# A graph network's first dense layers in three node blocks of 418 columns in place of four of 314

## The chip, the core and the metric

The kernel runs on one core of a Trainium2 chip. The time is the device time of one execution in microseconds (us). Engines are named as the profile names them: PE is TensorE, PEld its weight loads, DVE VectorE, ACT ScalarE, POOL GpSimd, SP SyncE. Each engine runs its own list of instructions in order, and engines wait for each other by counters (semaphores).

## The reference

Two graph layers follow each other on 1250 nodes of 512 values and 20000 edges. The first is the one that the change touches:

```python
h = jnp.maximum(_layernorm(x, axis=-1), 0.0)
agg = jax.ops.segment_sum(h[src], dst, num_segments=N)
z = (1.0 + eps) * h + agg
z = jax.nn.relu(batch_norm(z @ W1 + b1, g1, be1))      # 512 -> 1024
z = jax.nn.relu(batch_norm(z @ W2 + b2, g2, be2))      # 1024 -> 512
x = x + (h + z)
```

`batch_norm` takes mean and variance of a feature over all nodes. The second layer normalises `x` again, forms for every edge a two-layer product of both end nodes and the edge's 64 attributes with `mish` behind each, sums the messages by target node, and ends in an update network over the nodes:

```python
h = mish(concatenate([h[src], h[dst], edge_attr]) @ W1 + b1)
agg = jax.ops.segment_sum(mish(h @ W2 + b2), dst, num_segments=N)
out = mish(concatenate([h, agg]) @ W3 + b3) @ W4 + b4
```

## The kernel before, in words

The program is written by hand, one list of instructions for each engine. Its stages in order of time: counts of the edges between each pair of nodes (to about 103 us of the span), the first layer's sum as a product with that count matrix (line 870, to 153.7), the first network's two products (line 952, 155 to 270), a short stretch to turn the result back to rows and normalise it, the products P and Q of the second layer (line 995, 280 to 338), the edge loop (to about 1050), and the update network.

In the first network features lie on partitions and nodes along the row, 1250 nodes padded to `NW` columns, cut in `BLOCKS` blocks of `BW` columns, each with a bank of PSUM of its own. Every factor is held as a high and a low part, so one product is three matmuls (high by low, low by high, high by high). `product_t` issues them. For the first output group of 128 features (o = 0) it goes by the inner dimension k, and for each k over all blocks, since its inputs are made one k after the other. For the others it takes one block after another, with all k in it, in two hardware loops. In the second product (4 outputs, 8 inner steps) `between` is called behind the first of the two loops: `transpose_back(o - 1)` turns the output before back to rows by ten transposes on PE (line 925), into banks 0 to 3.

ACT moves each finished block out of PSUM with its bias (`move_product`, L1190), takes the square root of a variance (L1180), and applies scale, shift and ReLU to a whole output (L1184). DVE takes the batch statistics of each moved block (`batch_norm`, L1539), sums them up (L1544), works out scale and shift in four small steps (L1549 to L1552), and behind the second block adds the transposed output before to `x` (`residual_early`, L1927). At the last output this call does more: ten statistics over the first 384 values of every row tile of `x` (L1936). Only then come the remaining blocks' statistics.

Hand-over from the first to the second product: the ReLU outputs are split by ACT (L1280, high) and DVE (L1909, low), and PE takes inner step k when the low part of k is there. Hand-over from the second product to rows: with no further output to hide it, the last output's move, statistics, scale, shift and ReLU (L1310, by blocks), its transposes (in groups of 2, 4 and 4 row tiles, `FILLS`), residual, row statistics (L1953, L1957) and normalisation (L1321) follow one another. PE runs 13 products whose result nobody reads before the first of these transposes, and 2, 4 and 7 further on (`idle_products`, L812).

The lines that set the order around the change:

```python
for o in range(1, on):
    for first, end in ((0, BLOCKS // 2), (BLOCKS // 2, BLOCKS)):
        with pe.Fori(first, end) as b:
            ...
        if between and first == 0:
            between(o - 1)
```

Of the kernel before, what the change touches and what calls it, by code (L numbers as in the profile page):

```python
# [17 lines left out]
ALU = mybir.AluOpType  # L18
# [8 lines left out]
P = 128  # L27
# [59 lines left out]
FINAL = EDGE_PAIRS - 1  # L87
assert EDGE_TILES == 2 * FINAL + 1 and FINAL % 2 == 0
SLOTS = 4
BLOCKS = 4  # L90

BW = -(-NODES // (2 * BLOCKS)) * 2
NW = BLOCKS * BW
assert NODES <= NW <= NP
LN_EPS = BN_EPS = 1e-5


# [17 lines left out]
def gnn_kernel(nc, x, src_cols, dst_cols, dst_rows, edge_attr_t, eps, cols, rows, w01, w02,  # L115
               w1, w2, w3, w4, out):
    ctx = ExitStack()
    with ctx:
# [59 lines left out]

        iota_at = place[0]
        IOTA, _ = sb("iota", [P, NP])  # L180
        XWORK_0, _ = sb("mish3_work_0", [P, 2, BW], at=iota_at)
        XWORK_1, _ = sb("mish3_work_1", [P, 2, BW], at=b2_at)
        XWORK = (XWORK_0[:, :, :], XWORK_1[:, :, :])
        assert place[0] <= nc.sbuf_usable_end

# [144 lines left out]
        UP_0, _ = sb("u_part_0", [P, 6, BW], at=wa_at + 4 * KD * DIM)  # L330
        UP_1, _ = sb("u_part_1", [P, 6, BW], at=wb_at + 4 * KD * DIM)
        UP_2, _ = sb("u_part_2", [P, 4, BW], at=rows_at)
        assert 4 * 6 * BW <= 4 * KD * DIM and 4 * 4 * BW <= 4 * 3 * DIM
# [122 lines left out]
        Z0_READY = (7, 7, 10, 12)  # L456
        SPREAD_ROWS = [(a, min(a + 512, NP)) for a in range(0, NP, 512)]
        MM_1 = 0
        FREE = 4
        MM_2 = BLOCKS * KH  # L460
        MM_PQ = MM_2 + BLOCKS * KD
        MM_UP = MM_PQ + 2 * NT
        MM_U = MM_UP + BLOCKS * KD
        TABLE_STORED = 16 * NT

        OUT_LAST = NT - 2
# [74 lines left out]
        def _(pool):  # L541
# [207 lines left out]
            def u_high(n):  # L749

                b, q = n // UPAIRS, n % UPAIRS
                at = (slice(2 * q, 2 * q + 2), slice(b * BW, (b + 1) * BW))
# [8 lines left out]


            pool.wait_ge(tr_done, TR_AG + NT)
            for n in range(UPAIRS * BLOCKS):
                u_high(n)
            for nt in range(OUT_LAST):
                finish(nt)
# [2 lines left out]
        def _(pe):  # L770
# [174 lines left out]
            def product_t(base, weights, acts, kn, on, ready, count, between=None):  # L945


                def terms(k, o, b):
                    bank = Z2[:, bass.ds(b, 1), 0:BW].rearrange("p o n -> p (o n)")
                    nodes = bass.ds(b * BW, BW)  # L950
                    for n, (w, a) in enumerate(((0, 1), (1, 0), (0, 0))):
                        mm = pe.matmul(bank, weights[w][:, k, o * P:(o + 1) * P], acts[a](k)[:, nodes],  # L952
                                       start=(k == 0 and n == 0), stop=(k == kn - 1 and n == 2), skip_group_check=True)
                    return mm

                for k in range(kn):
# [53 lines left out]
                pq(1, nt, q_moved, 0)  # L1010
            def u_terms(bank, high_w, low_w, high, low, o, b):

                nodes = slice(b * BW, (b + 1) * BW)
# [24 lines left out]
            def z2(s, j, k):  # L1038

                at, e = Z2[:, 2 * j + k, :], slice(k * P, (k + 1) * P)  # L1040
                if k == 0:
                    if after(s, 2):
                        pe.wait_ge(msg_full, s - 1)
                    else:
                        pe.wait_ge(up_moved, BLOCKS * KD)
# [51 lines left out]

            pe.wait_ge(w3a_lo, KD)
            pe.wait_ge(mm_moved, FREE + MM_PQ + NT)
            for b in range(BLOCKS):  # L1100
                for o in range(KD):
                    n = KD * b + o
                    if n == 2:
                        pe.wait_ge(q_moved, NT)
                    if n >= 4:
                        pe.wait_ge(up_moved, n - 3)
                    u_terms(Z2[:, n % 4, 0:BW], W3A_HI, W3A_LO, HT_HI, HT_LO, o, b)
# [17 lines left out]
            def y_product(nt):  # L1125

                if nt >= 4:
                    pe.wait_ge(y_moved, nt - 3)
                nodes = slice(nt * P, min((nt + 1) * P, NW))
                last_block = (nodes.stop - 1) // BW  # L1130
                for k in range(KD):
                    if k % 2 == 0:
                        pe.wait_ge(u_lo, UPAIRS * last_block + k // 2 + 1)
                    for n, (u, w) in enumerate(((U_LO, W4_HI), (U_HI, W4_LO), (U_HI, W4_HI))):
                        mm = pe.matmul(BANKS[0:nodes.stop - nodes.start, nt % 4, :], u[:, k, nodes], w[:, k, :],  # L1135
                                       start=(k == 0 and n == 0), stop=(k == KD - 1 and n == 2))
                mm.then_inc(y_done, 1)

            def u_product(b, q):


                pe.wait_ge(ag_lo, -(-(b + 1) * BW // P))
                if b > 0:
                    pe.wait_ge(u_bias, UPAIRS * (b - 1) + q + 1)
                for o in (2 * q, 2 * q + 1):
                    u_terms(Z2[:, o, 0:BW], W3B_HI, W3B_LO, AG_HI, AG_LO, o, b)

            def ag_t(nt):
                transpose_node(AGG, nt, ag_lo)
# [7 lines left out]
            u_product(0, 1)  # L1157
            ag_t(8)
            ag_t(9)
            for b in range(1, BLOCKS):  # L1160
                for q in range(UPAIRS):
                    u_product(b, q)
            pe.wait_ge(w4_lo, KD)
# [4 lines left out]
        def _(act):  # L1168
# [247 lines left out]
            for b in range(BLOCKS):  # L1416
                for o in range(KD):
                    n = KD * b + o
                    act.wait_ge(mm_done, MM_UP + n + 1)
                    if n == 12:  # L1420
                        act.wait_ge(rows_used, 2 * NT)
                    nc.scalar.activation(u_part(b, o)[:, 0, :], Z2[:, n % 4, 0:BW], ACT.Identity, bias=COLS[:, CB3 + o:CB3 + o + 1]).then_inc(up_moved, 1)
# [69 lines left out]
            u_log(0)  # L1492
            ag_high(9)
            u_inverse(0)
            for n in range(1, UPAIRS * BLOCKS):
                u_mish(n)
            for nt in range(NT):
                y_scale(nt)
# [2 lines left out]
        def _(dve):  # L1501
# [619 lines left out]
            dve.wait_ge(agg_done, SUMS1 + EDGE_GROUPS)  # L2121
            def u_at(n):
                b, q = n // UPAIRS, n % UPAIRS
                return slice(2 * q, 2 * q + 2), slice(b * BW, (b + 1) * BW)

            def u_start(n):

                b, q = n // UPAIRS, n % UPAIRS
                o, nodes = u_at(n)
                dve.wait_ge(mm_done, MM_U + KD * b + 2 * q + 2)  # L2130
                nc.vector.tensor_tensor(UT[:, o, nodes], Z2[:, o, 0:BW], u_part(b, 2 * q, 2), ALU.add).then_inc(u_bias, 1)

            def u_bound(n):

# [48 lines left out]
            u_bound(1)  # L2183
            ag_low(8)
            ag_low(9)
            for n in range(2, UPAIRS * BLOCKS):
# [56 lines left out]
```

## Time and profile before

| | us |
|---|---|
| median of three runs | 1128.69 |
| lowest and highest | 1127.28, 1129.93 |
| the profiled execution | 1129.61 |
| its span in the trace | 1127.6 |
| PE busy in it | 1066.4 |
| DVE, ACT, POOL busy | 871.6, 896.2, 656.1 |

The span is the stretch that the trace covers. The profiled execution's own time is 2.0 us longer than its span. PE is busy in 95% of the span. Shares of busy time are no limit by themselves: two matmuls in the pipeline overlap in the trace, since each is drawn from its start to the arrival of its last result, so the pace of PE is read from the distance of starts, not from the length of one.

### The profile page before, as it was taken

The numbers are of one execution on the slowest core, as the hardware profiler recorded it, in microseconds if no ns is written. First come the engines' busy times: TensorE is split into PE (matmuls) and PEld (weight loads), VectorE is DVE, ScalarE is ACT, GpSimd is POOL, SyncE is SP. The second block draws the span as 40 slices with busy tenths as digits, with TensorE's granted clock in tenths as the row PEclk, the third lists the DMA queues.
The fourth block names the chain that finished last, engine by engine and source line by source line (L and its number), as shares of the span: only waits on it lengthen the run. The fifth ranks groups of instructions, "written<-read, shape, count | busy, mean of one in ns | idle before, by whom it ended". The sixth has DMA issues, their size and how long they took to land.

```text
span 1127.6 us, 18568 instructions
## 1 busy us (share of the span) xinstructions
PE 1066.4 (95%) x5764; PEld 902.2 (80%) x5765; DVE 871.6 (77%) x1529; ACT 896.2 (79%) x1134; POOL 656.1 (58%) x549
## 2 busy tenths in 40 slices
PE   3568999999999999999999999999999999999997
PEld 1125889998888888888888888888888888888795
DVE  7999535536426388888889998998888888888786
ACT  5995745624503799999999999999999999999584
POOL 6765323002155576776888888888876677660227
PEclk9779999999999999999999999999999999999999
DMA  3003920301265386666666666666666666661002
GB/s 103 8 1 103 160 75 1 122 1 47 75 224 112 87 189 144 145 131 138 129 141 139 131 133 145 131 139 133 140 137 133 136 141 133 137 129 39 1 1 92
DMA packets 61087, 121.41 MB, mean 108 GB/s; under 512 B 7851, under 2 KB 18348, under 8 KB 60918
## 3 DMA queue, kind: packets, MB, share of 16 engines
q0 software_dynamic: 38048, 87.58, 38.3%
q1 hardware_dynamic: 22998, 33.32, 8.9%
q8 instruction: 21, 0.34, 0.1%
q14 instruction: 20, 0.16, 0.0%
HBM read 107.82 MB, written 7.80 MB: 103 GB/s over the span
## 4 chain that ended last, share of the span: by engine, by line
PE 86%; DVE 9%; ACT 2%; issue 2%; DVEq 1%; POOL 0%; ACTq 0%; POOLq 0%
PE banks L1054 12%; PE banks L1049 12%; PE banks L1050 12%; PE banks L952 10%; PE banks L1034 7%; PE banks L1074 6%; PE banks L1028 6%; PE banks L995 5%; PE banks L1016 4%; PE banks L870 4%; DVE edge_counts L1713 4%; PE banks L1047 3%; PE banks L1135 2%; DVE key_onehot L1660 1%; PE banks L925 1%
## 5 line engine op out<-in xcount | busy, mean ns | idle before, releaser
L688 POOL DMA_INDIRECT gather_pq<-q_table,dst x157 | 295.4, 1882 | 56.8 <-issue 47.5
L680 POOL DMA_INDIRECT gather_pq<-p_table,src x157 | 173.3, 1104 | 138.6 <-PE banks L1034 85.4
L1049 PE MATMUL banks<-w_lo,h_hi 128*128 128x512 f32 x620 | 241.5, 390 | 0.0
L1050 PE MATMUL banks<-w_hi,h_hi 128*128 128x512 f32 x620 | 241.3, 389 | 0.0
L1054 PE MATMUL banks<-w_hi,h_lo 128*128 128x512 f32 x620 | 166.2, 390 | 0.0
L1050 PEld LDWEIGHTS banks<-w_hi,h_hi 128*128 128x128 f32 x620 | 116.4, 188 | 24.8
L1054 PEld LDWEIGHTS banks<-w_hi,h_lo 128*128 128x128 f32 x620 | 116.4, 188 | 24.2
L2009 DVE SCALAR_TENSOR_TENSOR h_full<-mish_work,banks 128x512 f32<-128x512 f32 (+1 forms) x154 | 98.4, 681 | 46.6 <-ACT mish_work L1362 43.4
L1049 PEld LDWEIGHTS banks<-w_lo,h_hi 128*128 128x128 f32 x620 | 116.5, 188 | 21.9
L2034 DVE SCALAR_TENSOR_TENSOR message<-mish_work,banks 128x1024 f32<-128x1024 f32 x78 | 95.3, 1221 | 8.7 <-ACT mish_work L1386 0.7
L1350 ACT ACTIVATE mish_work<-banks 128x1024 f32<-128x1024 f32 (+1 forms) x77 | 78.6, 1021 | 26.4 <-PE banks L1034 26.3
L1034 PE MATMUL banks<-edge_attr_parts,we_hi 128*128 128x256 f32 (+1 forms) x316 | 94.6, 321 | 2.4 <-DVE edge_attr_parts L2002 2.4
L2044 DVE TENSOR_TENSOR message_lo<-message,message_hi 128x1024 fp32r<-128x1024 f32 x78 | 96.0, 1231 | 0.1
L1028 PE MATMUL banks<-ident,gather_pq 128*128 128x128 f32 x628 | 94.4, 272 | 0.3 <-DVE h_full L2009 0.2
L2023 DVE TENSOR_TENSOR h_lo<-h_full,h_hi 128x1024 fp32r<-128x1024 f32 (+1 forms) x77 | 93.3, 1211 | 0.0
L1382 ACT ACTIVATE mish_work<-mish_work 128x1024 f32<-128x1024 f32 (+1 forms) x79 | 83.4, 1055 | 2.5
L1028 PEld LDWEIGHTS banks<-ident,gather_pq 128*128 128x128 f32 x628 | 74.8, 140 | 11.1 <-DVE h_full L2009 0.6
L1358 ACT ACTIVATE mish_work<-mish_work 128x1024 f32<-128x1024 f32 (+1 forms) x77 | 81.4, 1057 | 2.4
L1354 ACT ACTIVATE mish_work<-mish_work 128x1024 f32<-128x1024 f32 (+1 forms) x77 | 81.3, 1056 | 2.5
L1386 ACT ACTIVATE mish_work<-mish_work 128x1024 f32<-128x1024 f32 (+1 forms) x79 | 83.1, 1052 | 0.1
L1378 ACT ACTIVATE mish_work<-mish_work 128x1024 f32<-128x1024 f32 (+1 forms) x79 | 82.4, 1044 | 0.1
L1034 PE MATMUL banks<-edge_attr_parts,we_lo 128*128 128x256 f32 (+1 forms) x316 | 81.8, 281 | 0.0
(269 smaller groups left out, 2686.2 us busy)
## 6 DMA issues: line engine op xcount, KB each, us to landing
edge_attr<-in_edge_attr_t SPq DMA_DIRECT2D x79, 128.0 KB, 3.5
x_nodes<-h_hi POOLq DMA_DIRECT2D x10, 256.0 KB, 13.4
x_nodes<-h_lo POOLq DMA_DIRECT2D x10, 256.0 KB, 7.9
p_table<-p_stage SPq DMA_DIRECT2D x10, 256.0 KB, 2.0
q_table<-agg_nodes SPq DMA_DIRECT2D x10, 256.0 KB, 3.9
gather_pq<-p_table,src POOLq DMA_INDIRECT x157, 3.9
gather_pq<-q_table,dst POOLq DMA_INDIRECT x157, 4.9
x_nodes<-in_x SPq DMA_DIRECT2D x3, 768.0 KB, 6.3
```

The lines of the kernel that those rows point to most:

```text
L680: nc.gpsimd.indirect_dma_start(GP[:, 2 * j + k, :], None, p_tab[:, :], bass.IndirectOffsetOnAxis(ap=SRC[:, 2 * s + k:2 * s + k + 1], axis= ...
L688: nc.gpsimd.indirect_dma_start(GP[:, 2 * j + k, :], None, q_tab[:, :], bass.IndirectOffsetOnAxis(ap=DST[:, 2 * s + k:2 * s + k + 1], axis= ...
L952: mm = pe.matmul(bank, weights[w][:, k, o * P:(o + 1) * P], acts[a](k)[:, nodes], start=(k == 0 and n == 0), stop=(k == kn - 1 and n == 2) ...
L1028: pe.matmul(Z1v[:, c, k * P:(k + 1) * P], GP[:, 2 * slot + k, c * P:(c + 1) * P], IDENT[:, :], is_transpose=True, skip_group_check=True, s ...
L1034: mm = pe.matmul(Z1v[:, c, 0:P * tiles(s)], w[:, c * P:(c + 1) * P], AT_R[:, j, 0:P * tiles(s)], skip_group_check=True, start=False, stop= ...
L1049: pe.matmul(at, h_high(s, j)[:, c, e], W2_LO[:, c, :], start=False, stop=False)
L1050: pe.matmul(at, h_high(s, j)[:, c, e], W2_HI[:, c, :], start=False, stop=False)
L1054: mm = pe.matmul(at, h_low(s, j)[:, c, e], W2_HI[:, c, :], start=False, stop=(c == KD - 1))
L2009: nc.vector.scalar_tensor_tensor(h_full_of(s)[:, at[0], at[1]], z1_work(s)[:, at[0], at[1]], -0.5, Z1v[:, at[0], at[1]], ALU.add, ALU.mult ...
L2023: nc.vector.tensor_tensor(h_low(s, j)[:, :, 0:P * tiles(s)], h_full_of(s)[:, :, 0:P * tiles(s)], h_high(s, j)[:, :, 0:P * tiles(s)].bitcas ...
L2034: nc.vector.scalar_tensor_tensor(MSG[:, :, :], EB[:, :, :], -0.5, z2_out(s, j), ALU.add, ALU.mult).then_inc(msg_full, 1)
L2044: nc.vector.tensor_tensor(MSG_LO[:, :, :], MSG[:, :, :], MSG_HI[:, :, :].bitcast(F32), ALU.subtract).then_inc(msg_lo, 1)
```

## The change

`BLOCKS` is now 3, `BW` 418 and `NW` 1254 for the first network and its input. The update network at the end keeps four blocks of 314 under new names, `UBLOCKS` and `UBW`. The two hardware loops of an output cover blocks 0 and 1, and block 2; the transposes stand between them. ACT's early split of a hidden output, which `BLOCKS // 2` places, now comes behind block 1.

```diff
-BLOCKS = 4
-
-BW = -(-NODES // (2 * BLOCKS)) * 2
+BLOCKS, UBLOCKS = 3, 4
+BW, UBW = (-(-NODES // (2 * n)) * 2 for n in (BLOCKS, UBLOCKS))
 NW = BLOCKS * BW
-assert NODES <= NW <= NP
+assert NODES <= NW <= UBLOCKS * UBW <= NP
...
-        FREE = 4
+        FREE = BLOCKS
...
-        MM_U = MM_UP + BLOCKS * KD
+        MM_U = MM_UP + UBLOCKS * KD
...
-                    for first, end in ((0, BLOCKS // 2), (BLOCKS // 2, BLOCKS)):
+                    for first, end in ((0, BLOCKS - 1), (BLOCKS - 1, BLOCKS)):
                         with pe.Fori(first, end) as b:
```

The remaining lines of the diff put `UBW` and `UBLOCKS` where the update network used `BW` and `BLOCKS`. Lines of the changed kernel stand one further down.

On DVE, at the last output of the second product, behind the scale and shift of the output before. `act_t` is the second product's result, `x_nodes` the rows. Before:

```order
L1539 BN_STATS bn_stats<-act_t 128x6 x2
L1927 TENSOR_TENSOR x_nodes<-x_nodes,banks 128x2x128
L1927 TENSOR_TENSOR x_nodes<-x_nodes,banks 128x4x128 x2
L1936 BN_STATS stats<-x_nodes 128x6 x10
L1539 BN_STATS bn_stats<-act_t 128x6 x2
L1544 BN_AGGR bn_mean_var<-bn_stats 128x2
L1549 RECIPROCAL tmp<-tmp 128x1
```

In the changed kernel:

```order
L1540 BN_STATS bn_stats<-act_t 128x6 x2
L1928 TENSOR_TENSOR x_nodes<-x_nodes,banks 128x2x128
L1928 TENSOR_TENSOR x_nodes<-x_nodes,banks 128x4x128 x2
L1937 BN_STATS stats<-x_nodes 128x6 x10
L1540 BN_STATS bn_stats<-act_t 128x6
L1545 BN_AGGR bn_mean_var<-bn_stats 128x2
L1550 RECIPROCAL tmp<-tmp 128x1
```

The order stays: residual and ten row statistics behind the second block's statistics. Behind them stand one block's statistics where there were two, so the run of thirteen instructions is now directly ahead of the last block.

On ACT, at the same place: the last moves, the splitting of the next layer's weights, the square root, and the ReLU by blocks. Before:

```order
L1190 ACTIVATE act_t<-banks,cols 128x314 x3
L1297 CAST w_hi<-weights_a 128x512 x2
L1180 ACTIVATE tmp<-bn_mean_var,consts 128x1
L1297 CAST w_hi<-weights_a 128x512 x2
L1310 ACTIVATE act_t<-act_t,bn_shift,bn_scale 128x314 x4
```

In the changed kernel:

```order
L1191 ACTIVATE act_t<-banks,cols 128x418 x2
L1298 CAST w_hi<-weights_a 128x512 x2
L1181 ACTIVATE tmp<-bn_mean_var,consts 128x1
L1298 CAST w_hi<-weights_a 128x512 x2
L1311 ACTIVATE act_t<-act_t,bn_shift,bn_scale 128x418 x3
```

One move and one ReLU piece fewer stand there, and each of the others is a third wider.

## Rows read from the trace of the kernel before

**Rows 1.** The page, part 1: busy time, share, instructions, by engine.

```profile
PE 1066.4 (95%) x5764; PEld 902.2 (80%) x5765; DVE 871.6 (77%) x1529; ACT 896.2 (79%) x1134; POOL 656.1 (58%) x549
```

**Rows 2.** Chain of waits by time, 150:345: start us, us, engine and line, count.

```profile
155.35 60.93 PE banks L952 x420
...
216.29 15.95 PE banks L952 x108
...
233.34 13.83 PE banks L952 x96
...
305.99 32.71 PE banks L995 x144
```

**Rows 3.** Timeline of PE, 152:155.5: start us, us, operation, shapes.

```profile
152.14 0.27 PE L870 MATMUL banks<-counts_hi,h_hi 128*128 128x232 f32 x1
...
152.58 0.40 PE L870 MATMUL banks<-counts_hi,h_hi 128*128 128x512 f32 x1
...
153.05 0.39 PE L870 MATMUL banks<-counts_hi,h_hi 128*128 128x512 f32 x1
...
155.35 0.38 PE L952 MATMUL banks<-z_t_lo,w_hi 128*128 128x314 f32 x1 [1.67 <-DVE z_t_lo L1869]
```

**Rows 4.** Groups by form, 155:273 and 155:275: count, busy us, mean ns, idle before.

```profile
L1539 DVE BATCH_NORM_STATS2 bn_stats<-hidden_t 128x6 f32<-128x314 f32 x24 | 11.2, 482 | 11.7 <-ACT hidden_t L1190 11.7
...
L1936 DVE BATCH_NORM_STATS2 stats<-x_nodes 128x6 f32<-128x384 f32 x10 | 4.7, 545 | 0.0
...
L1190 ACT ACTIVATE hidden_t<-banks,cols 128x314 f32<-128x314 f32 x32 | 16.2, 519 | 23.8 <-PE banks L952 23.8
L1184 ACT ACTIVATE hidden_t<-hidden_t,bn_shift,bn_scale 128x1256 f32<-128x1256 f32 x8 | 11.5, 1434 | 2.4 <-DVE bn_shift L1552 2.4
```

**Rows 5.** Timeline between the two products, 204:232, PE and DVE.

```profile
210.85 0.30 PE L952 MATMUL banks<-hidden_lo,w_hi 128*128 128x314 f32 x1
...
214.78 7.12 DVE L1909 TENSOR_TENSOR hidden_lo<-hidden_t,hidden_hi 128x1256 fp32r<-128x1256 f32 x5
```

**Rows 6.** Timeline, 262:264.8: the last output's transposes on PE.

```profile
261.92 1.25 PE L925 MATMUL banks<-ident,act_t 128*128 128x128 f32 x10
```

**Rows 7.** Timeline of DVE, 262:276.

```profile
262.67 0.49 DVE L1539 BATCH_NORM_STATS2 bn_stats<-act_t 128x6 f32<-128x314 f32 x1 [2.08 <-ACT act_t L1190]
...
264.71 4.70 DVE L1936 BATCH_NORM_STATS2 stats<-x_nodes 128x6 f32<-128x384 f32 x10
269.33 0.47 DVE L1539 BATCH_NORM_STATS2 bn_stats<-act_t 128x6 f32<-128x314 f32 x1
270.65 0.48 DVE L1539 BATCH_NORM_STATS2 bn_stats<-act_t 128x6 f32<-128x308 f32 x1 [0.85 <-ACT act_t L1190]
271.16 0.26 DVE L1544 BATCH_NORM_AGGREGATE bn_mean_var<-bn_stats 128x2 f32<-128x24 f32 x1
```

**Rows 8.** Timeline of ACT, 269:276.

```profile
270.09 0.52 ACT L1190 ACTIVATE act_t<-banks,cols 128x314 f32<-128x314 f32 x1 [2.92 <-PE banks L952]
...
271.54 0.29 ACT L1180 ACTIVATE tmp<-bn_mean_var,consts 128x1 f32<-128x1 f32 x1
...
272.77 2.27 ACT L1310 ACTIVATE act_t<-act_t,bn_shift,bn_scale 128x314 f32<-128x314 f32 x4
```

**Rows 9.** Timeline of PE, 269:281.

```profile
269.89 3.16 PE L812 MATMUL banks<-b_parts,ones 128*128 128x512 f32 x13
273.47 0.44 PE L925 MATMUL banks<-ident,act_t 128*128 128x128 f32 x2 [0.42 <-ACT act_t L1310]
```

**Rows 10.** Stretches of PE: length, busy (instructions), granted clock, DMA share, GB/s.

```profile
155.30:158.70 3.40, 3.35 (x23) 1.00 1.00 351
...
353.50:356.90 3.40, 3.40 (x16) 0.50 0.94 227
356.90:360.30 3.40, 3.40 (x25) 1.00 0.73 170
```

**Rows 11.** Timeline of PE, 349:357: the hole ahead of them.

```profile
352.10 0.39 PE L1034 MATMUL banks<-edge_attr_parts,we_hi 128*128 128x256 f32 x1 [2.44 <-DVE edge_attr_parts L2002]
```

More of the change, by code:

```diff
@@ L180, in gnn_kernel @@
         IOTA, _ = sb("iota", [P, NP])
-        XWORK_0, _ = sb("mish3_work_0", [P, 2, BW], at=iota_at)
-        XWORK_1, _ = sb("mish3_work_1", [P, 2, BW], at=b2_at)
+        XWORK_0, _ = sb("mish3_work_0", [P, 2, UBW], at=iota_at)
+        XWORK_1, _ = sb("mish3_work_1", [P, 2, UBW], at=b2_at)
         XWORK = (XWORK_0[:, :, :], XWORK_1[:, :, :])
@@ L329, in gnn_kernel @@
         W3B_HI, W3B_LO = W3_HI[:, 0, :, :], W3_LO[:, 0, :, :]
[L330 to L333, printed above, removed]
+        UP_0, _ = sb("u_part_0", [P, 6, UBW], at=wa_at + 4 * KD * DIM)
+        UP_1, _ = sb("u_part_1", [P, 6, UBW], at=wb_at + 4 * KD * DIM)
+        UP_2, _ = sb("u_part_2", [P, 4, UBW], at=rows_at)
+        assert 4 * 6 * UBW <= 4 * KD * DIM and 4 * 4 * UBW <= 4 * 3 * DIM
         UT, _ = sb("u_t", [P, KD, NP], at=t1_at)
@@ L751, in u_high @@
                 b, q = n // UPAIRS, n % UPAIRS
-                at = (slice(2 * q, 2 * q + 2), slice(b * BW, (b + 1) * BW))
+                at = (slice(2 * q, 2 * q + 2), slice(b * UBW, (b + 1) * UBW))
                 pool.wait_ge(u_ready, n + 1)
@@ L763, in _ @@
             pool.wait_ge(tr_done, TR_AG + NT)
-            for n in range(UPAIRS * BLOCKS):
+            for n in range(UPAIRS * UBLOCKS):
                 u_high(n)
@@ L1011, in u_terms @@
             def u_terms(bank, high_w, low_w, high, low, o, b):
-                nodes = slice(b * BW, (b + 1) * BW)
+                nodes = slice(b * UBW, (b + 1) * UBW)
                 for k in range(KD):
@@ L1044, in z2 @@
                     else:
-                        pe.wait_ge(up_moved, BLOCKS * KD)
+                        pe.wait_ge(up_moved, UBLOCKS * KD)
                     pe.wait_ge(h_hi, s + 1)
@@ L1099, in _ @@
             pe.wait_ge(mm_moved, FREE + MM_PQ + NT)
-            for b in range(BLOCKS):
+            for b in range(UBLOCKS):
                 for o in range(KD):
@@ L1106, in _ @@
                         pe.wait_ge(up_moved, n - 3)
-                    u_terms(Z2[:, n % 4, 0:BW], W3A_HI, W3A_LO, HT_HI, HT_LO, o, b)
+                    u_terms(Z2[:, n % 4, 0:UBW], W3A_HI, W3A_LO, HT_HI, HT_LO, o, b)
                     if n in Z1_BEHIND:
@@ L1128, in y_product @@
                     pe.wait_ge(y_moved, nt - 3)
-                nodes = slice(nt * P, min((nt + 1) * P, NW))
-                last_block = (nodes.stop - 1) // BW
+                nodes = slice(nt * P, min((nt + 1) * P, UBLOCKS * UBW))
+                last_block = (nodes.stop - 1) // UBW
                 for k in range(KD):
@@ L1139, in u_product @@
             def u_product(b, q):
-                pe.wait_ge(ag_lo, -(-(b + 1) * BW // P))
+                pe.wait_ge(ag_lo, -(-(b + 1) * UBW // P))
                 if b > 0:
@@ L1145, in u_product @@
                 for o in (2 * q, 2 * q + 1):
-                    u_terms(Z2[:, o, 0:BW], W3B_HI, W3B_LO, AG_HI, AG_LO, o, b)
+                    u_terms(Z2[:, o, 0:UBW], W3B_HI, W3B_LO, AG_HI, AG_LO, o, b)
             def ag_t(nt):
@@ L1159, in _ @@
             ag_t(9)
-            for b in range(1, BLOCKS):
+            for b in range(1, UBLOCKS):
                 for q in range(UPAIRS):
@@ L1415, in _ @@
             act.wait_ge(q_stored, TABLE_STORED)
-            for b in range(BLOCKS):
+            for b in range(UBLOCKS):
                 for o in range(KD):
@@ L1421, in _ @@
                         act.wait_ge(rows_used, 2 * NT)
-                    nc.scalar.activation(u_part(b, o)[:, 0, :], Z2[:, n % 4, 0:BW], ACT.Identity, bias=COLS[:, CB3 + o:CB3 + o + 1]).then_inc(up_moved, 1)
+                    nc.scalar.activation(u_part(b, o)[:, 0, :], Z2[:, n % 4, 0:UBW], ACT.Identity, bias=COLS[:, CB3 + o:CB3 + o + 1]).then_inc(up_moved, 1)
                     for s, first in enumerate(Z1_BEHIND):
@@ L1494, in _ @@
             u_inverse(0)
-            for n in range(1, UPAIRS * BLOCKS):
+            for n in range(1, UPAIRS * UBLOCKS):
                 u_mish(n)
@@ L2123, in u_at @@
                 b, q = n // UPAIRS, n % UPAIRS
-                return slice(2 * q, 2 * q + 2), slice(b * BW, (b + 1) * BW)
+                return slice(2 * q, 2 * q + 2), slice(b * UBW, (b + 1) * UBW)
             def u_start(n):
@@ L2130, in u_start @@
                 dve.wait_ge(mm_done, MM_U + KD * b + 2 * q + 2)
-                nc.vector.tensor_tensor(UT[:, o, nodes], Z2[:, o, 0:BW], u_part(b, 2 * q, 2), ALU.add).then_inc(u_bias, 1)
+                nc.vector.tensor_tensor(UT[:, o, nodes], Z2[:, o, 0:UBW], u_part(b, 2 * q, 2), ALU.add).then_inc(u_bias, 1)
             def u_bound(n):
@@ L2185, in _ @@
             ag_low(9)
-            for n in range(2, UPAIRS * BLOCKS):
+            for n in range(2, UPAIRS * UBLOCKS):
                 u_end(n - 2)
```

## The prediction

> **What bounds the kernel now.** I read the page first: PE is busy for 95% of the span [rows 1], so the question in each stage is only whether PE waits. Then the chain of waits over the changed stage, where the reader is to see that it runs through PE's line 952 almost without a break from 155.35 to about 270 [rows 2]. Inside the two products PE is the bound; DVE and ACT lie beside it. Three places are different: the start (PE waited 1.67 us for the last stage's result [rows 3]), the seam between the products, and the end, where nothing is left for PE and a chain of ACT and DVE steps decides. So the change is weighed as pace of the matmuls, plus what happens at the seam and at the end. Behind them P and Q follow with PE in the chain [rows 2], so a shift at the end is handed on whole.
>
> **The pace.** The columns stay: four blocks of 314 are 1256, three of 418 are 1254. The matmuls fall. First product: 8 outputs x 4 inner steps x 3 terms is 96 for each block, second: 4 x 8 x 3, again 96. So 192 groups of four matmuls become groups of three. One of 314 columns takes 13.83 / 96 = 144.1 ns from start to start, one of 512 takes 32.71 / 144 = 227.2 ns [rows 2]. At the granted full clock of 2.4 GHz the columns alone would be 130.8 and 213.3 ns; both sizes pay 13 to 14 ns beside them. No row has 418 columns. On the line between the two, 418 lies at 144.1 + 104 x (227.2 - 144.1) / 198 = 187.7 ns. A group is then 563.1 in place of 576.4 ns, 13.3 ns less, and 192 of them save **2.5 us**. The other end is line 870: 152.14 to 152.58 holds four of 232 columns, 110 ns each, 152.58 to 153.05 two of 512, 235 ns each [rows 3]. A straight line through these gives 193 ns at 418, a group of 579 ns, and the change would lose 0.5 us. I take the first, since lines 952 and 995 share the form (two parts by two parts, all in one bank for a whole run) while 870 goes from bank to bank. Range of the term: gain 2.7 (all of the fixed part plus two columns) to loss 0.5. Smaller: the input's last part is 230 wide, not 232, in 80 matmuls at (235 - 110) / 280 = 0.45 ns a column, 0.07 us gained. The hardware loops have one pass fewer for each output; the 96 matmuls of four passes ran at 144.1 ns, passes included, so I give that nothing.
>
> The Trainium skill, "TensorE: Matmul & The Clock Gate", section "Back-to-back issue gap", gives N / 2.4 GHz + 2.5 ns as the isolated distance when warm. By that the fixed part of a matmul would be a fifth of what these rows show, and 192 groups would save 192 x (2.5 + 0.8) ns, an estimate of 0.6 us, in place of 2.5. The trace differs with its 144.1 and 227.2 ns, and I go by the trace.
>
> **Banks.** Three banks serve where four did. The tightest use is at o = 1, where block 0 is wanted right behind o = 0. Its last matmul starts seven starts earlier, 1.3 us, its move starts 0.34 us behind that start (as 269.89 less 0.14 and 270.09 show [rows 8, 9]) and takes 0.62, so about 0.3 us are left. This cover is work of PE on the other two blocks; were it gone, it would cost up to 0.3 us twice. Elsewhere a bank has two blocks of at least 2.2 us as cover. Nothing for this. ACT's early split, about as long as the ReLU of 1434 ns [rows 4], follows this behind block 1 and delays the third move by about 1 us in two outputs, and that bank is not wanted for 4 us. Nothing either.
>
> **Wider pieces.** A move of 314 columns takes 519 ns, the ReLU over 1256 takes 1434 [rows 4], so 0.97 ns a column, and a piece of 418 takes 0.10 us more. Statistics: 482 ns at 314, 545 at 384 [rows 4], 0.90 ns a column, 0.09 to 0.10 us more at 418. While PE is the bound this is hidden. At seam and end it is not.
>
> **The seam.** PE starts the second product at 210.85 [rows 5] and reaches inner step 3 after 36 matmuls, at 216.04 by its pace. It really starts there at 216.29 [rows 2], because the fourth low part, the first of the five from 214.78 at 7.12 / 5 = 1.42 us each [rows 5], ends at 216.20. So PE lost 0.25 us. In the new kernel PE is there after 27 x 187.7 = 5.07 us, 0.12 earlier, and the low part comes 0.10 later, since the last move is longer and the split queues behind it on ACT. PE loses 0.47 in place of 0.25: **0.22 us lost**. The later low parts come each 1.42 us, PE wants one each 1.69, so they catch up.
>
> **The end.** This is where most is given back. Take as zero the start of the last output's transposes, 261.92 [rows 6]. DVE takes the second block's statistics at +0.75, then three residuals and from +2.79 to +7.49 the ten row statistics [rows 7]. The third block's statistics wait behind them until +7.41 and the fourth's start at +8.73, with DVE free [rows 7]: today the batch fits beneath two blocks of PE, 48 matmuls. In the new kernel it has to fit beneath one, 24 matmuls.
> New, from the same zero: PE takes 1.05 us for transposes (7.97 to the idle products [rows 9] less 48 x 0.1441) and 24 x 0.1877 = 4.51 for the last block, so it is done at +5.56 (call it E). The last move starts at E + 0.20 as today [rows 8, 9], and its statistics could start 0.56 + 0.10 later, at +6.42. DVE's batch starts 0.20 later than today (a wider move and wider statistics ahead) and frees DVE at +7.61. The last statistics wait **1.19 us**, in order on DVE. Behind them nothing is hidden. Today the square root starts 0.89 us after them [rows 7, 8]; the statistics are 0.10 longer, and some 0.07 falls away, since the root stands behind ACT's weight split and starts 0.12 after the sum's end at 271.42 [rows 7, 8], and that split will be long over. So the root starts at +8.53. The ReLU follows 1.23 us later [rows 8], and the transposes 0.70 after that [rows 8, 9], plus 0.10 for its wider first piece. Sum: transposes at +10.56, that is E + 5.00. Today they start at 273.47, 3.58 us after 269.89 [rows 9]. **1.42 us lost.** From there the path goes in order on DVE, with the same instructions. The second and third groups of transposes come earlier, as three pieces of ReLU are shorter than four, but DVE is not ready for them: no gain. POOL's weight split starts by the same signal, later by as much, and stays beneath the row statistics and the normalisation, which are later by as much too.
>
> **Sum.** -2.5 - 0.07 + 0.22 + 1.42 = -0.93 us. Made against the profiled execution's 1129.61 it gives 1128.68 (its span of 1127.6 would be 1126.7). That execution lies 0.9 us above the median of the three, 1128.69, and the same difference taken off the median gives **1127.8 us**. What can be told from no change by measuring this kernel is 0.2%, or 2.3 us, more than the sum.
>
> **Rivals.** *The gain comes whole* (chance 0.12). Were DVE's batch no obstacle, only the pace and the wider pieces would count, -2.5 - 0.07 + 0.22 + 0.25: 1126.6. For it speaks that PE's busy share is 95%; against it that DVE's list is in order and the batch stands ahead of the last block by the listing of both kernels.
> *The clock falls at the end* (0.18), the one that ends slower. PE's 13 idle products end 3.16 us after E today, and the hole behind them is 0.42 us [rows 9]. It would grow to 5.00 - 3.16 = 1.84 us. The trace has a hole of 1.67 us after which the clock stayed at 1.00 [rows 3, 10] and one of 2.44 us [rows 11] after which it was granted at 0.50, 1.2 GHz, for 3.4 us, in which PE started 16 matmuls where 25 followed in the next stretch [rows 10]. The new hole lies between. The work near it is partly idle products and transposes, but the seven idle products ahead of P are on the path. Price up to 1.7 us, half of 3.4: 1127.8 + 1.7 = 1129.5. It decides from a hole somewhere between 1.67 and 2.44 us on; against it speaks that 1.84 is nearer to the harmless one.
> *The pace is proportional to columns* (0.10). If what stands beside the columns grows with them (144.1 / 314 = 0.459 ns a column), a group saves 0.9 ns, or by line 870 loses 3, and seam and end still cost their 1.64: +1.4 to +2.1, 1130.1 to 1130.8. The small fixed part of the page named above would come out near it, at -0.6 - 0.07 + 1.64, or 1129.7.
> *The forecast* has 0.55. Left over, 0.05, is a stall that I do not see, in the banks first.
>
> **How the numbers follow.** The forecast's own range is 1127.0 to 1128.6. The range that is to hold 8 in 10 takes in the clock rival and most of the whole gain, and about 1 us for the runs' own scatter (1127.28 to 1129.93): 1126.0 to 1130.2. Faster by over 0.2% (below 1126.4) needs the whole gain and some luck: 0.13. Slower by over 0.2% (above 1130.9) needs pace and clock both wrong: 0.06. Within: 0.81.
>
> **What would show it.** In the changed profile: line 953 at 187 to 188 ns from start to start (192 would be the third rival); no wait of PE for ACT's move; the first wait for the low part at inner step 3 of about 0.5 us; ten statistics of x ending about 1.9 us after the last of line 953, the last block's statistics right behind them with no idle time before; PE idle for about 1.8 us ahead of the first transposes; the granted clock there at 1.00 (0.50 is the second rival). The prediction is wrong if DVE stands idle ahead of the last statistics, or if the end takes 3.8 us as today.

## The result and the profile after

The changed kernel takes 1131.95 us (median of 14 runs, 1129.99 to 1133.29) beside 1128.90 us for the kernel before (14 runs): ratio 1.0027, 95% interval 1.0019 to 1.0035. It is 3.05 us slower, by 0.27%, which lies above the predicted range of 1126.0 to 1130.2. The profiled execution took 1131.98 us, with a span of 1129.9.

The trace says where the time went. The table takes each stage from the start of its first matmul to the start of its last, or of the next stage's first.

| us | before | after | forecast | found |
|---|---|---|---|---|
| first layer's sum (L870) | 50.69 | 50.96 | -0.07 | +0.27 |
| first network (L952) | 114.40 | 113.80 | -2.28 | -0.60 |
| its end, to the first product P (L995) | 10.51 | 11.70 | +1.42 | +1.19 |
| products P and Q | 58.26 | 58.29 | 0 | +0.03 |
| edge loop (L1049), first to last | 673.86 | 675.96 | 0 | +2.10 |
| update network | 70.31 | 70.32 | 0 | +0.01 |

The rows add up to 3.00 us, beside 3.05 between the medians. Two stretches are left out, because they change from one profile to the next whatever the kernel. The counting stage ends, and the first layer's sum starts, at 102.59 us before and at 103.23 after, and between 101.3 and 103.4 in the profiles of all kernels below but e7, which adds work there. Between Q and the edge loop the profile of before has the clock at 0.50 for 3.4 us [rows 10], and that of after has not, which shortens this one profile by 1.37 us. Of the kernels below, e1, e2, e5, e6, e7, e10 and e11 have that fall, e3, e8, e9 and e12 do not.

**Two thirds of the loss lie where no line of code was changed**, in the edge loop.

The page says of PE what it said before [rows 1], and gives no hint of this:

```profile
PE 1066.8 (94%) x5572; PEld 894.8 (79%) x5573; DVE 871.1 (77%) x1517; ACT 894.1 (79%) x1121; POOL 657.6 (58%) x549
```

The chain of waits of the changed kernel, 150 to 345 us (start, length, engine and line, count), answers to [rows 2]:

```profile
156.25 55.33 PE banks L953 x288
...
212.12 1.25 ACT hidden_hi L1281
...
215.51 1.39 DVE hidden_lo L1910
216.95 18.04 PE banks L953 x93
...
236.08 13.77 PE banks L953 x72
...
250.94 13.79 PE banks L953 x72
...
307.48 32.74 PE banks L996 x144
```

The piece at 236.08 has the pace: 13.77 / 72 = 191.3 ns for 418 columns, where the sum had 187.7. In the middle the chain leaves PE, as forecast: the low part of inner step 3 is late. The waits of PE's weight loads between 205 and 235 us (total, times, longest), first of the kernel before, then of the changed one:

```profile
PEld banks L952 <- DVE hidden_lo L1909: 0.3, 1, 0.3
```

```profile
PEld banks L953 <- DVE hidden_lo L1910: 0.7, 2, 0.4
```

The end, on DVE and ACT of the changed kernel (timeline; idle time and its releaser in brackets), beside [rows 7, 8]:

```profile
265.39 0.60 DVE L1540 BATCH_NORM_STATS2 bn_stats<-act_t 128x6 f32<-128x418 f32 x1 [3.11 <-ACT act_t L1191]
...
267.54 4.70 DVE L1937 BATCH_NORM_STATS2 stats<-x_nodes 128x6 f32<-128x384 f32 x10
272.15 0.58 DVE L1540 BATCH_NORM_STATS2 bn_stats<-act_t 128x6 f32<-128x414 f32 x1
```

```profile
274.26 1.99 ACT L1311 ACTIVATE act_t<-act_t,bn_shift,bn_scale 128x418 f32<-128x418 f32 x3
```

The last block's statistics follow the ten row statistics with no idle time, although ACT had moved their block by 271.05. On PE (beside [rows 9]) and in the stretches with the granted clock (third number from the right; beside [rows 10]):

```profile
270.25 3.13 PE L813 MATMUL banks<-b_parts,ones 128*128 128x512 f32 x13
275.05 0.44 PE L926 MATMUL banks<-ident,act_t 128*128 128x128 f32 x2 [1.67 <-ACT act_t L1311]
```

```profile
272.50:275.05 2.55, 0.88 (x5) 1.00 1.01 386
275.05:278.50 3.45, 2.84 (x16) 1.00 0.21 48
```

PE was idle for 1.67 us ahead of the first transposes, and the granted clock stayed at 1.00, the level of 2.4 GHz. It stayed there too behind a longer hole, the one that answers to [rows 11], here with the stretch behind it:

```profile
353.63 0.39 PE L1035 MATMUL banks<-edge_attr_parts,we_hi 128*128 128x256 f32 x1 [2.59 <-DVE edge_attr_parts L2003]
```

```profile
353.90:357.30 3.40, 3.40 (x28) 1.00 1.00 195
```

A hole of 2.44 us was followed by 0.50 in the kernel before [rows 10, 11], and one of 2.59 us was not in the changed one. So the length of the hole does not decide by itself.

The edge loop. One of its lines, first and last start, of the kernel before and of the changed one:

```profile
L1049 PE MATMUL banks<-w_lo,h_hi x620: 387/389/398, 383.0 to 1049.2; 128*128 128x512 f32 x155
```

```profile
L1050 PE MATMUL banks<-w_lo,h_hi x620: 387/389/398, 383.2 to 1051.4; 128*128 128x512 f32 x155
```

666.2 us have become 668.2, and the single matmul is no longer than it was (387/389/398 ns, lowest, median, highest). What PE's weight loads wait for in 376:1049, before and after:

```profile
PEld banks L1028 <- DVE h_full L2009: 0.6, 1, 0.6
PEld banks L1028 <- issue: 0.5, 1, 0.5
```

```profile
PEld banks L1029 <- issue: 6.0, 20, 0.5
PEld banks L1029 <- DVE h_full L2010: 4.2, 18, 0.6
```

And DVE's sequencer, the register load in its loop (lowest, median, highest ns), before and after:

```profile
L1565 DVEq TENSOR_LOAD <-tile_range x39: 744/749/760, 388.5 to 1048.4; - x39
```

```profile
L1566 DVEq TENSOR_LOAD <-tile_range x38: 744/754/875, 388.6 to 1035.7; - x38
```

It hardly ever varied before; now it takes up to 875 ns. In 17 passes it stands at 799 to 875, the 3rd to the 9th and the 27th to the 36th, and PE has its 18 waits for DVE's `h_full`. Over the 35 passes from 409 to 1018 us the loads took 26.2 us before and 27.7 after, so they alone are 1.5 us longer. So DVE's sequencer is slower there, with the same instructions. The clock is no part of it: it was granted at 1.00 through the whole loop in both profiles.

### The profile page after: what moved, and what is told of

Same layout as the page of the kernel before. It is cut to its first block, busy times and chain, and to the rows that moved or that the text cites. A ratio compares the mean times of both kernels' runs of the same rounds, so it can differ in the third digit from the quotient of the medians.

```text
span 1129.9 us, 17891 instructions
## 1 busy us (share of the span) xinstructions
PE 1066.8 (94%) x5572; PEld 894.8 (79%) x5573; DVE 871.1 (77%) x1517; ACT 894.1 (79%) x1121; POOL 657.6 (58%) x549
## 4 chain that ended last, share of the span: by engine, by line
PE 85%; DVE 10%; ACT 2%; issue 2%; DVEq 1%; POOL 0%; ACTq 0%; POOLq 0%
PE banks L1050 12%; PE banks L1055 12%; PE banks L1051 12%; PE banks L953 9%; PE banks L1035 7%; PE banks L1075 6%; PE banks L1029 6%; PE banks L996 5%; PE banks L871 4%; PE banks L1017 4%; DVE edge_counts L1714 4%; PE banks L1048 3%; PE banks L1136 2%; DVE key_onehot L1661 1%; PE banks L926 1%
## 5 line engine op out<-in xcount | busy, mean ns | idle before, releaser
L681 POOL DMA_INDIRECT gather_pq<-p_table,src x157 | 176.7, 1125 | 137.0 <-PE banks L1035 83.8
L1351 ACT ACTIVATE mish_work<-banks 128x1024 f32<-128x1024 f32 (+1 forms) x77 | 78.6, 1021 | 28.4 <-PE banks L1035 28.4
L1029 PEld LDWEIGHTS banks<-ident,gather_pq 128*128 128x128 f32 x628 | 72.4, 140 | 15.2 <-issue 6.0
L1375 ACT ACTIVATE mish_work<-banks 128x1024 f32<-128x1024 f32 (+1 forms) x79 | 79.2, 1002 | 3.3 <-PE banks L1055 3.3
```

The lines of the kernel that those rows point to most:

```text
L681: nc.gpsimd.indirect_dma_start(GP[:, 2 * j + k, :], None, p_tab[:, :], bass.IndirectOffsetOnAxis(ap=SRC[:, 2 * s + k:2 * s + k + 1], axis= ...
L1029: pe.matmul(Z1v[:, c, k * P:(k + 1) * P], GP[:, 2 * slot + k, c * P:(c + 1) * P], IDENT[:, :], is_transpose=True, skip_group_check=True, s ...
```

## Experiments

Two things could make an untouched loop slower: where its data lie (the statistics buffer shrank from 24 to 18 numbers an output, and all buffers behind it moved), or where its instructions lie in an engine's list (ahead of the loop DVE has 12 instructions fewer, ACT 13, and PE, in the output groups that are written out one by one, 36 matmuls with their weight loads). Lengths of the stages in us, from the same starts as above; medians are of the runs, beside those of the kernel before on the same chip. e6, e7, e11 and e12 ran once, for their profile, so that their times are no basis for a ratio:

| | L870 | first network | end | edge loop | median (before) | ratio |
|---|---|---|---|---|---|---|
| before | 50.69 | 114.40 | 10.51 | 673.86 | 1128.90 | 1 |
| after | 50.96 | 113.80 | 11.70 | 675.96 | 1131.95 (1128.90) | 1.0027 |
| e1 | 50.69 | 114.38 | 10.52 | 673.90 | 1129.08 (1129.03) | 1.0002 |
| e2 | 50.96 | 113.77 | 11.71 | 675.81 | 1132.12 (1129.03) | 1.0035 |
| e3 | 50.95 | 113.78 | 10.67 | 676.11 | 1130.36 (1129.03) | 1.0014 |
| e5 | 50.95 | 114.18 | 11.68 | 673.84 | 1129.74 (1128.95) | 1.0006 |
| e6 | 50.96 | 113.77 | 11.69 | 675.85 | 1132.49, one run | |
| e7 | 50.96 | 114.02 | 11.70 | 676.03 | 1139.04, one run | |
| e8 | 50.98 | 113.77 | 10.66 | 673.84 | 1128.07 (1128.95) | 0.9992 |
| e9 | 50.72 | 113.12 | 11.73 | 676.12 | 1130.86 (1129.06) | 1.0015 |
| e10 | 50.73 | 112.35 | 10.66 | 673.76 | 1127.54 (1129.06) | 0.9986 |
| e11 | 50.69 | | | 676.85 | 1144.64, one run | |
| e12 | 50.68 | | | 673.79 | 1139.64, one run | |

**e1 and e2, the place of the buffers.** e1 is the kernel before, with the buffers where the change puts them:

```diff
-        BSTATS, _ = sb("bn_stats", [P, KH, 6 * BLOCKS])
+        place[0] += 4 * KH * 18
...
+        BSTATS, _ = sb("bn_stats", [P, KH, 6 * BLOCKS])
```

> The kernel before with four blocks of 314, but every buffer behind the batch statistics moved down by 192 bytes, to where the changed kernel has it (the statistics themselves stand at the end). The changed kernel's profile loses 2.1 us in the edge loop, whose code is the same. If the place of the buffers (the iota row, the small tables) does that, this kernel is 1.5 to 2.5 us slower than before and its edge loop (first product of line 1049's group to its last) takes about 676 us. If not, it is within 0.5 us of before and the loop takes about 674.

Measured: edge loop 673.90, ratio 1.0002 (0.9992 to 1.0013). e2 is the changed kernel with a statistics buffer as wide as before:

```diff
-        BSTATS, _ = sb("bn_stats", [P, KH, 6 * BLOCKS])
+        BSTATS_WIDE, _ = sb("bn_stats", [P, KH, 6 * UBLOCKS])
+        BSTATS = BSTATS_WIDE[:, :, 0:6 * BLOCKS]
```

> The changed kernel with a statistics buffer as wide as before, so that no later buffer moves. By the theory of the place it gains 2 us on the changed kernel and is about 1 us slower than before (ratio 1.001), loop 674 us. If the place is not the cause, it is like the changed kernel, 3 us slower than before (ratio 1.0027), loop 676 us.

Measured: 675.81, ratio 1.0035 (1.0024 to 1.0047). The place of the buffers is not the cause.

**e3, the end.** The changed kernel with seven of the ten row statistics ahead, and three where DVE waits for ACT anyway, behind the last scale and shift:

```diff
-                    for nt in range(NT):
...
+                    early_rows(0, ROWS_AHEAD)
...
+            early_rows(ROWS_AHEAD, NT)
```

> The changed kernel with seven of the ten row statistics ahead of the last block's statistics and three behind the last scale and shift. If these ten hold the last block back by 1.2 us, the time from the last of the second product's matmuls to the first of P falls from 11.7 us to 10.6, and the kernel is about 1.1 us faster than the changed one. If the end is longer for another reason (wider pieces, transposes), it falls by less than 0.4 us.

Measured: the end takes 10.67 for 11.70 us, the ratio is 1.0014 (1.0004 to 1.0024). DVE and PE of e3:

```profile
267.34 3.32 DVE L1934 BATCH_NORM_STATS2 stats<-x_nodes 128x6 f32<-128x384 f32 x7
270.89 0.59 DVE L1540 BATCH_NORM_STATS2 bn_stats<-act_t 128x6 f32<-128x414 f32 x1 [0.23 <-ACT act_t L1191]
...
272.85 1.47 DVE L1934 BATCH_NORM_STATS2 stats<-x_nodes 128x6 f32<-128x384 f32 x3
```

```profile
273.80 0.44 PE L926 MATMUL banks<-ident,act_t 128*128 128x128 f32 x2 [0.62 <-ACT act_t L1311]
```

Now DVE is free 0.23 us before the last block is moved, where in the changed kernel the block waited for DVE. The predicted mechanism is shown; the edge loop stays at 676.11, so the two are separate.

**e4, the pace by itself.** Only groups of matmuls of the form of L952 at sixteen widths and places, the rest of the computation left out.

> Leaves the whole computation out and runs only groups of matmuls (high and low part by rounded values) at sixteen widths and offsets, all else idle. The changed kernel's matmuls of 418 columns start 191.3 ns apart in the mean, not 187.7. If that is a matter of where rows begin or end in steps of 64 bytes (16 columns), 416 columns at multiples of 416 run at 186 to 187 ns and 418 at 191. If it is the neighbours (ACT and DVE at work), 418 runs at 187.7 here, as on the straight line. If every width that is no multiple of 128 or so has a rest of its own, 416 and 420 stand at 190 too, and 314 above its line.

Measured, mean ns from start to start, blocks side by side as in the kernel:

| columns | 256 | 314 | 320 | 384 | 416 | 418 | 420 | 424 | 448 | 480 |
|---|---|---|---|---|---|---|---|---|---|---|
| ns | 119.9 | 144.2 | 146.7 | 173.4 | 187.8 | 191.0 | 190.3 | 192.2 | 202.9 | 215.3 |
| less columns / 2.4 GHz | 13.2 | 13.4 | 13.3 | 13.4 | 14.4 | 16.8 | 15.3 | 15.5 | 16.2 | 15.3 |

With all blocks at offset 0, 418 takes 189.9 ns. The chain over the stretches of 416 and of 418 columns:

```profile
76.20 13.51 PE banks L175 x72
```

```profile
89.71 13.75 PE banks L175 x72
```

So the 191 ns of the network are the matmul's own, not the work of its neighbours, of which this kernel has none. The line from 314 to 512 columns (13 to 14 ns beside the columns at both ends) holds up to 384. Between 416 and 480 a matmul pays 1 to 3.5 ns more than that, and 418, of all widths tried, the most. These means mix paces: group by group (twelve matmuls into one bank) this one trace has 186.5 to 189.8 ns at 416 columns, where the line has 186.7, 189.5 to 192.5 at 418, and 186.7 to 191.9 at 420. So a difference of 1 ns between two widths says little; the 3.2 between 416 and 418 is clear. For 418 about 1 ns goes with the offset (189.9 with all blocks at 0) and the rest with the width; why is open.

**e5, e6, e7, the place in the list.** Small operations whose result nobody reads move the edge loop of one engine down its list: e5 twelve one-number copies on DVE ahead of the second `batch_norm` and e6 thirteen on ACT, which puts each loop back to where it stood; e7 98 matmuls of two columns on PE in the first stage, which need not be PE's old place.

```diff
+            for k in range(12):
+                nc.vector.tensor_copy(PAD[0:1, 16 + k:17 + k], CONST[0:1, 1:2])
```

> The changed kernel with twelve copies of one number on DVE ahead of the second product's statistics, where DVE is idle, so that DVE's edge loop stands at the same place of its instruction list as before (the change took twelve statistics out of the list). If the edge loop's extra 2.1 us comes from where DVE's loop stands in its instruction list, the loop takes 673.9 us again, DVE's register load of line 1565 takes 0.75 us throughout, and the kernel is 2 us faster than the changed one. If the cause is ACT's list or PE's, or the state in which the loop begins, the loop still takes about 676.

> The changed kernel with thirteen copies of one number on ACT ahead of the second product's moves, so that ACT's edge loop stands where it stood before in its list. Loop 673.9 us if ACT's place is the cause, about 676 if DVE's or PE's is.

> The changed kernel with 98 matmuls of two columns on PE in the counting stage, where PE is mostly idle, which brings PE's edge loop back to about the place in its list that it had before. Loop 673.9 us if PE's place is the cause, about 676 if not.

Measured: e5 673.84 us, e6 675.85, e7 676.03. With e5 the median falls to 1129.74, ratio 1.0006 (0.9997 to 1.0015). PE's waits in e5's loop and DVE's register load read like those of before:

```profile
PEld banks L1030 <- DVE h_full L2013: 0.6, 1, 0.6
PEld banks L1030 <- issue: 0.6, 2, 0.5
```

```profile
L1567 DVEq TENSOR_LOAD <-tile_range x38: 745/750/764, 390.1 to 1035.1; - x38
```

The cause is DVE's list: twelve instructions that do nothing useful take 2.1 us out of the loop, with PE's and ACT's lists left as in the changed kernel. e6 has the same extra buffer as e5 and stays slow, so it is not the buffer. (e7's total means nothing for this, since its own matmuls lengthen the first stage.)

**e11, e12, is it the place modulo 256?** The Trainium skill, "Runtime: NRT & Kernel Launch", section "Instruction fetch mechanics", says that an engine's instruction memory is refilled in blocks of 256 instructions and that a taken branch to a target outside the two blocks at hand has to fetch it. It also calls block crossings mostly hidden. If blocks of 256 are what counts, the kernel before must get slow with its loop 244 instructions further down (12 less than 256) and stay fast with 256.

```diff
+            for k in range(244):
+                nc.vector.tensor_copy(PAD[0:1, k:k + 1], CONST[0:1, 1:2])
```

> The kernel before with 244 one-number copies on VectorE ahead of the second normalization, which puts its edge loop 244 instructions further down in VectorE's list: a whole number of 256 further than in the changed kernel, where the loop took 676.0 us. Theory (the place modulo 256 instructions decides): the edge loop takes 675.5 to 676.1 us and the register load at its head 0.80 to 0.88 us in many steps. Rival (not the place, but that twelve statistics had gone or what they stood beside): 673.9 us and 0.75 us. Only the edge loop is read; the copies themselves lengthen the part ahead of it.

> The kernel before with 256 such copies at the same place, the control of the kernel with 244: the same load on VectorE ahead of the loop, but the loop stands at the same place modulo 256 instructions as in the kernel before. Theory: edge loop 673.8 to 674.0 us, register load 0.75 us. If the number of instructions ahead or any large shift slows the loop: about 676 us, as with 244.

Measured: e11 676.85 us, e12 673.79. PE's waits in e11, then in e12:

```profile
PEld banks L1029 <- issue: 6.5, 20, 0.5
PEld banks L1029 <- DVE h_full L2012: 4.7, 18, 0.6
```

```profile
PEld banks L1029 <- DVE h_full L2012: 0.6, 1, 0.6
PEld banks L1029 <- issue: 0.6, 2, 0.5
```

The register load, e11 and e12:

```profile
L1566 DVEq TENSOR_LOAD <-tile_range x38: 744/757/985, 400.5 to 1048.5; - x38
```

```profile
L1566 DVEq TENSOR_LOAD <-tile_range x38: 744/749/764, 398.5 to 1043.4; - x38
```

e11 has the changed kernel's waits, 20 and 18 of them, with four blocks of 314 columns, and its load is slow in the same passes. Twelve copies more, and they are gone. e11 came 0.75 us above its expected interval, and why is not known; the verdict does not hang on it. With e5 this settles that the place of DVE's loop in its list decides, and that the effect is back after 256 instructions; a period that divides 256 would fit these runs as well. What DVE's sequencer waits for is open. A fetch of instructions in every slow pass would fit the block length that the Trainium skill gives, but the records do not support it: the trace has the packets of two instruction queues (q8 and q14), and from 425 to 570 and from 820 to 1010 us of the changed kernel, where the slow passes are, there is none. From 376 to 1070 us both kernels have the same 11 of them. Whether these two queues are all that carry DVE's instructions no run shows. Why just these passes are slow is open too.

**e8, the end and the place together.**

> The changed kernel with both: seven row statistics ahead and three behind the last block's, and DVE's twelve copies. If the end's 1.1 us and the loop's 2.1 us have these two causes, they add up: 1132.0 - 1.1 - 2.1 = 1128.8 us, level with before (ratio 0.999 to 1.0005). If the loop's time has another cause, it is like the split alone, 1130.4.

Measured: end 10.66, loop 673.84, 1128.07 us, ratio 0.9992 (0.9983 to 1.0001). In the stages the two effects add up; the median came 0.7 us below the expected one, within what the runs scatter.

**e9 and e10, 416 columns.** Blocks of 416, 416 and 418 columns, with the last block of every output written out on PE in place of its hardware loop of one pass:

```diff
+BW = 416
+LAST_W = NODES - (BLOCKS - 1) * BW
+NW = NODES
...
+def width(b):
+    return LAST_W if isinstance(b, int) and b == BLOCKS - 1 else BW
```

> The changed kernel with blocks of 416, 416 and 418 columns in place of three of 418; all else as in the changed kernel. Theory (the matmul's own length jumps above 416 columns: 187.8 ns at 416 and 191.0 ns at 418 where the products of the first network were timed by themselves): 128 of the 192 groups get 3.2 ns x 4 shorter, 1.6 us, so that the first network takes about 112.1 us from its first matmul to its last for 113.8, and the whole about 1130.3 us beside a changed kernel at 1131.95. Rival (191 ns came of what runs beside the matmuls in the first network, stores and loads of activations): 113.8 us and 1131.9. The edge loop stays at 676 us by both.

Measured: the chain of e9 has a piece with all three blocks in it,

```profile
234.21 13.52 PE banks L959 x72
```

187.8 ns each where the changed kernel has 191.3. (Two blocks of 192 matmuls at 3.2 ns are 1.23 us; the expectation counted 1.6, too much.) But the first network shrank by only 0.68: a stall in the first product, of a kind to which the prediction gave nothing, took 0.76 of it (55.02 us from its first matmul to its last, where e10 has 54.26). DVE, POOL and PE of e9:

```profile
171.59 0.16 DVE L1560 RECIPROCAL tmp<-tmp 128x1 f32<-128x1 f32 x1 [1.65 <-ACT tmp L1191]
171.79 4.88 DVE L1561 TENSOR_TENSOR bn_scale<-tmp,cols 128x1 f32<-128x1 f32 x1
176.70 0.16 DVE L1562 TENSOR_TENSOR tmp<-bn_mean_var,bn_scale 128x1 f32<-128x1 f32 x1
```

```profile
166.59 10.06 POOL L669 TENSOR_TENSOR w_lo<-weights_b,w_hi 128x512 fp32r<-128x512 f32 x8
```

```profile
180.21 0.46 PE L959 MATMUL banks<-z_t_lo,w_hi 128*128 128x418 f32 x1 [0.50 <-ACT hidden_t L1201]
```

A product of two single columns, 0.16 us elsewhere, took 4.88 us and ended with POOL's weight split. The ReLU and the moves behind it on ACT came late, and PE found the third block's bank not yet empty. e10 adds e3's split and e5's copies:

> The three-block kernel with all three findings together: blocks of 416, 416 and 418 columns, seven of the ten row statistics ahead of the last scale and shift and three behind, and twelve one-number copies on VectorE ahead of the second normalization, so that VectorE's edge loop stands where it stood in its list of instructions. If the three add up: first network 112.1 us for 113.8, end 10.7 for 11.7, edge loop 673.8 for 676.0, that is 1128.07 (the split and the copies alone) less 1.7, 1126.4 us, 0.998 of the kernel before. If the shorter matmuls only meet a later wait at the seams: 1128.0, 0.999.

Measured: 1127.54 us, ratio 0.9986 (0.9977 to 0.9996), the fastest of all, by 0.14% faster than before. Its profile has no such stall, and its first network takes 112.35 us, 1.42 less than e8's and 2.05 less than before. That is a little more than the 1.23 counted, for the last block too, still 418 wide but now at offset 832, became faster (in the first product 189.8 ns for 191.4). The expected 1126.4 was not reached: the stages account for about 1.9 us beside the kernel before, and the medians show 1.5.

## Why the prediction was wrong, point by point

The sum had -0.93 us and 3.05 came, about 4 us more. Two steps failed: the sum gave the edge loop nothing, and it cost 2.10, and the pace of 418 columns was read off a straight line, which promised 2.5 us where 0.5 came, so that the first network missed its forecast by 1.68. The first layer's sum adds 0.34, and the end was 0.23 better than forecast.

- **The pace**, the term of -2.5 us, was mis-sized. The step that failed is "on the line between the two, 418 lies at 187.7 ns". It takes 191.0 by itself and 191.3 in the kernel, so that a group is 573 to 574 ns in place of 576.4, and 192 groups save about 0.5 us. With the seam that leaves 0.2 to 0.3 us of the network's -0.60 that no term explains. The other end of the term (193 ns, from L870) was the nearer one. The reason given for setting it aside, that L870 goes from bank to bank, was sound as a doubt but no evidence for the line. The line itself was not wrong in its ends (314 takes 144.2 in e4), only between them. The prediction named 192 ns as the sign of the third rival, and that is about what came.
- **The seam**: a first wait of about 0.5 us at inner step 3, 0.22 more than before, was forecast. By the prediction's own count (start of the step less the matmuls ahead of it at their pace) it is 216.95 - 211.41 - 27 x 0.1913 = 0.37 us for 0.25. The weight loads have a second wait that it did not have, 0.7 in total for 0.3. Right in kind, and within 0.2 us.
- **The banks**: right for the changed kernel, whose matmuls wait for no move. But the cover is thinner than the prediction had it: by 0.50 us in e9 and 0.15 in e5, PE did wait for a move, when DVE stood behind POOL. In the kernel before three of the four small steps between statistics and ReLU already take 0.61, 1.22 and 1.22 us at this place, where they take 0.16 elsewhere, and the prediction did not read them.
- **The end**: +1.42 forecast, +1.19 found, by the mechanism named, and shown by e3. The transposes came 275.05 - 270.25 = 4.80 us after the idle products' start, where 5.00 was forecast and 3.58 was the time before. Counted from the start of the transposes (264.55 us), DVE began its batch at +2.99 and was free at +7.60, as the sum had it; but PE was done only at +5.70, not +5.56, since its last block took 4.69 us, not 4.51. So 0.14 of the 0.20 is the error of the pace again, and no merit of this term.
- **The clock rival** (0.18) did not occur: the hole was 1.67 us, 1.84 forecast, and the clock stayed at 1.00. Its condition, that the length of the hole decides somewhere between 1.67 and 2.44 us, does not hold as it stands: the same profile has a hole of 2.59 us with the clock at 1.00 behind it.
- **The third rival** (0.10), a pace in proportion to the columns with seam and end still to pay, was the nearest: 1130.1 to 1130.8. The network and its end together give +0.59, where this rival had +1.4 to +2.1, for the groups still save a little. The small fixed part by the Trainium skill, "TensorE: Matmul & The Clock Gate", section "Back-to-back issue gap", came close in its result (an estimate of -0.6 for the pace), not in its reason: the trace has 13 to 17 ns beside the columns at every width, not 2.5.
- **The edge loop**: no term of the sum and no rival had it. All steps took for granted that a stage whose code stays keeps its time. +2.10 us, more than the rest together, came of twelve statistics fewer on DVE in the first network, which ends 100 us ahead of the loop. Without it the change would be at about +0.9 (e5: +0.79, 1.0006): no difference by the prediction's 0.2%, and inside its range, but with the pace still wrong.
- **The first layer's sum**: +0.27 where -0.07 was forecast. It is there in every kernel with a last part 230 wide (50.95 to 50.98) and not with 232 (50.68 to 50.69) or 226 (50.72 to 50.73). So it goes with the width again, but what makes 230 dearer than either is open.

## What to carry to other kernels

A matmul's pace is not to be interpolated over a gap of widths when a gain of a few ns hangs on it: time the very width, and its neighbours (here 416 for 418 gave 1.4 us). An edit that drops or adds instructions on an engine moves all that it runs later; if a hardware loop further on gets slower with its code unchanged, shift it by a few idle instructions before anything else is believed. Work that is put ahead of a wait in an engine's ordered list must fit beneath what is left of the other engine's work, and it has to be measured again when the pieces change.

## What was not expected of the hardware

- **The same DVE loop took 673.8 or 675.8 to 676.9 us** by its place in DVE's list, and the same again 256 instructions further down, with a register load of 0.75 or up to 0.99 us, and no packet of an instruction queue in the slow stretches.
- **418 columns cost 191.0 ns, 416 cost 187.8 and 420 cost 190.3**, blocks side by side, in the mean of 72 matmuls: the time beside the columns is 13.2 to 13.4 ns up to 384 and 14.4 to 16.8 from 416 to 480.
- **A DVE step with two inputs of one column waited up to 4.88 us while POOL split weights**, which takes 10.06 / 8 = 1.26 us an instruction, while RECIPROCAL, with one input, passed in 0.16 in the midst of it. The Trainium skill, "SBUF — State Buffer", section "SBUF: two separate sides", has it that these two engines share a port pair as an exclusive lock, which a DVE operation with two SBUF inputs needs. The trace agrees in which operation is held up; the wait was longer than one POOL instruction, about four.
